# A scan layer with a mixture-of-experts layer: more places in the back phase, and a new order of the engines' work

## The reference

```python
h = layernorm(x) * (1 + ca) + sa
u = causal_conv(h, conv_w) + conv_b            # 4 taps, per channel
x_dbl = u @ xproj_w.T                          # dt (128), B (16), C (16)
delta = softplus(dt @ dtproj_w.T + dtproj_b)
# for each of 16 states n, in order of time:
#   h_n = exp(delta * A_n) * h_n + delta * B_n * u ;  y += C_n * h_n
x1 = x + ga * (y + u * D_skip)
h2 = layernorm(x1) * (1 + cb) + sb
# the router picks 2 of 8 experts for each row; scores = softmax of the two logits
out = x1 + gb * sum over the two experts of score_e * (silu(h2 @ Wup_e.T + bup_e) @ Wdown_e.T + bdown_e)
```

## Time and profile before

| | us |
|---|---|
| median of the three runs | 1313.03 |
| the profiled execution | 1310.42 |
| its span | 1308.7 |
| last scan of the front phase begins | about 1132 |
| last PE instruction ends | 1292.5 |

### The profile page before, as it was taken

How to read it: one execution, slowest core, us unless ns; L and a number is a source line. 1 busy time by engine, 2 the same in 40 slices (tenths; PEclk the granted TensorE clock), 3 DMA queues, 4 the chain that set the end, 5 groups by cost and what they waited for, 6 DMA issues and landing times. The chain is left out here.

```text
span 1308.7 us, 19847 instructions
## 1 busy us (share of the span) xinstructions
PE 1120.7 (86%) x5556; PEld 753.5 (58%) x5556; DVE 1110.2 (85%) x1562; ACT 877.6 (67%) x1684; POOL 916.8 (70%) x788
## 2 busy tenths in 40 slices
PE   8979778767769988898889998989889698999994
PEld 4467655445546656565557674656566465666551
DVE  4898899999988999899789998999889998853145
ACT  4864887948658975897598669976788474453231
POOL 2576686788778878888898767988887877423211
PEclk9999969757979999999999998999999789999997
DMA  6576443123224325233444521442541345785575
GB/s 213 182 262 218 121 158 101 49 73 139 82 93 121 129 66 153 94 130 96 140 119 132 145 64 60 143 137 72 155 121 66 115 143 183 232 285 185 153 232 171
DMA packets 104739, 181.02 MB, mean 138 GB/s; under 512 B 24864, under 2 KB 33056, under 8 KB 103608
## 3 DMA queue, kind: packets, MB, share of 16 engines
q1 hardware_dynamic: 91432, 141.33, 35.2%
q0 software_dynamic: 13200, 38.43, 7.7%
HBM read 116.34 MB, written 68.86 MB: 142 GB/s over the span
## 5 line engine op out<-in xcount | busy, mean ns | idle before, releaser
L1247 POOL TENSOR_TENSOR DB<-DU,BR 128x1024 f32<-128x1024 f32 x222 | 523.3, 2365 | 125.2 <-DVE H L1677 107.8
L2014 PE MATMUL pb<-ID,H 128*128 128x128 f32 x2048 | 323.8, 294 | 86.8 <-DVE ACC L1702 63.5
L1465 ACT ACTIVATE pb<-DELP,AN 128x512 f32<-128x512 f32 x448 | 305.7, 687 | 135.5 <-DVE H L1677 127.0
L1702 DVE SCALAR_TENSOR_TENSOR ACC<-pb,CTM,ACC 128x512 f32<-128x512 f32 x512 | 373.5, 730 | 13.9 <-PE pb L2014 13.4
L2014 PEld LDWEIGHTS pb<-ID,H 128*128 128x128 f32 x2048 | 254.2, 151 | 173.5 <-DVE ACC L1702 67.6
L1677 DVE TENSOR_TENSOR_SCAN H<-pb,DB 128x512 f32<-128x512 f32 x256 | 310.9, 1215 | 35.1 <-ACT pb L1465 17.3
L1677 DVE TENSOR_TENSOR_SCAN H<-pb,ST,DB 128x512 f32<-128x512 f32 x192 | 244.9, 1275 | 12.4 <-ACT pb L1465 9.1
L1232 POOL DMA_INDIRECT ydr<-YO,SCR x85 | 89.9, 1058 | 145.6 <-ACT YO L1547 129.7
L1547 ACT ACTIVATE YO<-pb,SCR 128x512 f32<-128x512 f32 x85 | 58.1, 683 | 71.5 <-PE pb L2117 71.1
L2087 PE MATMUL pb<-WU,XTS 128*128 x340 | 99.5, 417 | 0.0
L2112 PE MATMUL pb<-WD,GT 128*128 x170 | 98.4, 661 | 0.0
(11 more groups left out here) (251 smaller groups left out, 1731.9 us busy)
## 6 DMA issues: line engine op xcount, KB each, us to landing
BR<-bscr SPq DMA_DIRECT2D x112, 256.0 KB
XS<-xdr SPq DMA_DIRECT2D x85, 256.0 KB
DU<-ydr SPq DMA_DIRECT2D x64, 256.0 KB
xdr<-ZZ SPq DMA_DIRECT2D x37, 264.0 KB, 5.3
ACC<-in_x SPq DMA_DIRECT2D x16, 512.0 KB, 3.5
DU<-in_x SPq DMA_DIRECT2D x7, 1024.0 KB, 5.6
x1s<-ACC SPq DMA_DIRECT2D x24, 256.0 KB, 2.2
DELP<-x1s SPq DMA_DIRECT2D x24, 256.0 KB, 3.5
```

The source lines that it names most:

```text
L1247: eng.tensor_tensor(DB[:, i % NDB:i % NDB + 2], DU[:, c % 2, r:r + 2], BR[:, n % 2:n % 2 + 1].to_broadcast([128, 2, CT]), ALU.mult).then_i ...
L1465: eng.activation(DA[i % NDA][:], DEL[:, c % 2, r], ACT.Exp, scale=AN[:, r, n:n + 1]).then_inc(S["da"], 1)
L1702: eng.scalar_tensor_tensor(out=acc, in0=banks[bank_of["flip", c, n, r]][:], scalar=1.0 if n < 0 else CTM[:, c % 2, j, st:st + 1], in1=acc, ...
L2014: t = eng.transpose(b[:, dt * 128:dt * 128 + 128], src[:, dt, r * 128:r * 128 + 128], ID[:])
```

## The change

The rows get four places in place of two, and x1 gets eight in place of four; the new places are in the half of `DU` and `DEL` that belongs to chunk 7. A first use of a new place waits for the last `dbu` or `da` of chunk 7; later uses wait for `fin` of block b - 4 and `out` of block b - 8. Loads and stores of an x1 place now count on one semaphore. No instruction on an engine is added or removed.

```diff
         def x1_tile(g, t):
...
-            return DEL[:, (NC - 2) % 2, back_no(g, t) % 4]
+            r = back_no(g, t) % 8
+            return DEL[:, x1_chunk(r) % 2, r % 4]
         def z_tile(g, t, way):
-            return DU[:, (NC - 2) % 2, 2 * (back_no(g, t) % 2) + way]
+            r = back_no(g, t) % 4
+            return DU[:, z_chunk(r) % 2, 2 * (r % 2) + way]
         def turn_of_z(g, t):
-            return S[f"d_g{back_no(g, t) % 2}"], back_no(g, t) // 2
+            return S[f"d_g{back_no(g, t) % 4}"], back_no(g, t) // 4
         def turn_of(g, t):
             r = back_no(g, t)
-            return S[f"d_v{r % 4}"], S[f"d_p{r % 4}"], r // 4
+            return S[f"d_p{r % 8}"], sum(32 if x < 4 * (NC - 2) else 16 for x in range(r % 8, r, 8))
...
-                        eng.wait_ge(S["fin"], b - 1)
+                        eng.wait_ge(S["fin"], b - 3)
                     elif way == 0:
-                        eng.wait_ge(S["dbu"], slot(NC - 2, NS - 1, 3) + 1)
+                        eng.wait_ge(S["dbu"], slot(z_chunk(b), NS - 1, 3) + 1)
...
-                        eng.wait_ge(S["da"], slot(NC - 2, NS - 1, 3) + 1)
+                        eng.wait_ge(S["da"], slot(x1_chunk(back_no(g, t)), NS - 1, 3) + 1)
```

More of the change, by code:

```diff
@@ L74 @@
[L74 to L79, removed]
@@ L230 @@
-        "out": (15832, 15864, 16023, 16166, 16413, 16479, 16541, 16606, 16750, 16839, 16928, 17036, 17144, 17267, 17346, 17472,
[5 rows of a table removed]
+        "del": (-4, -3, 1852, 1865, 1938, 1991, 3640, 3651, 3662, 3725, 5712, 5756, 5769, 5782, 8053, 8062, 8089, 8135, 9980,
[5 rows of a table added]
+        "gbt": (175,),
+        "gbm": (6,),
+        "gbk": (-30,),
+        "gbb": (181,),
+        "gbe": (24,),
+        "gbs": (23,),
+        "bdh": (151,),
+        "bdl": (178,),
+        "gbl": (175, 181, 16710, 17603),
+        "dg2": (10,),
@@ new lines @@
+        "rowz": (232, 260),
+        "rowy": (238, 244, 250, 267, 273, 279),
+        "rcq": (237, 314),
+        "rt": (777, 873),
+        "mod": (766, 862),
+        "ldw": (329, 339, 492, 641, 782, 939, 1093, 1253),
[7 rows of a table added]
+        "skx": (174, 177, 179, 183),
+        "skp": (185, 187, 189, 191),
+        "skc": (89, 115, 138, 144),
+        "flip_": (2154, 2162, 2170, 2173, 4202, 4211, 4213, 4222, 6246, 6252, 6263, 6265, 8300, 8303, 8310, 8312, 10345, 10354,
+        10357, 10366, 12396, 12398, 12405, 12407, 14438, 14442, 14446, 14455),
@@ L236 @@
+        "out": (15918, 15922, 16401, 16437, 16724, 16743, 16762, 16774, 16998, 17041, 17181, 17200, 17315, 17395, 17545, 17615,
[5 rows of a table added]
 }
@@ L264 @@
+    "cpe": "6324324426464434644422262223",
+    "skx": "2563",
+    "dtr": "4366623",
+    "ftr": "32334334643443632234433263643443",
+    "r1": "2333643344623446",
+    "r2": "4342246344223246",
+    "hb": "42336442322463224334336626632323",
+    "rk": "343346424",
+    "xt": "2333344336464336242232224462666623643446366266442662246333642432324424262423463423636",
+    "gt": "66362333622466266443464322243463636336264242",
 }
@@ L693, in adaln_kernel @@
                      "d_bdn", "d_xa0", "d_xa1", "d_xp", "d_dtp", "d_bw", "d_br0", "d_br1", "d_gs",
-                     "d_gb", "d_w", "d_zi", "d_sc", "d_xl0", "d_xl1", "d_xl2", "d_xl3", "d_zr", "d_y0", "d_y1", "d_y2", *(f"d_{x}{r}" for x, n in (("g", 2), ("v", 4), ("p", 4)) for r in range(n)), "d_x10", "d_x11",
+                     "d_gb", "d_w", "d_zi", "d_sc", "d_xl0", "d_xl1", "d_xl2", "d_xl3", "d_zr", "d_y0", "d_y1", "d_y2", *(f"d_{x}{r}" for x, n in (("g", 4), ("p", 8)) for r in range(n)), "d_x10", "d_x11",
                      "d_x12", "d_x13"):
@@ L772, in pair_end, with x1_chunk, z_chunk @@
             return tile_no(g, tiles_of(g, p - pair_no(g, 0))[-1])
+        def x1_chunk(r):
+            return NC - 2 if r < 4 else NC - 1
+        def z_chunk(r):
+            return NC - 2 if r < 2 else NC - 1
         def x1_tile(g, t):
@@ L1001, in _ @@
                     cs, j = tokens(g)[t]
-                    loaded, stored, turn = turn_of(g, t)
-                    if turn:
-                        eng.wait_ge(stored, 16 * turn)
+                    moved, before = turn_of(g, t)
+                    if before:
+                        eng.wait_ge(moved, before)
                     else:
-                        eng.wait_ge(S["da"], slot(NC - 2, NS - 1, 3) + 1)
+                        eng.wait_ge(S["da"], slot(x1_chunk(back_no(g, t)), NS - 1, 3) + 1)
                     eng.wait_ge(S[f"d_x1{2 * (cs % 2) + j}"], 16 * (cs // 2 + 1))
-                    eng.dma_start(x1_tile(g, t), x1s[rows_of(g, t), :]).then_inc(loaded, 16)
+                    eng.dma_start(x1_tile(g, t), x1s[rows_of(g, t), :]).then_inc(moved, 16)
                 elif what == "out":
@@ L1011, in _ @@
                     eng.wait_ge(S["fin"], back_no(g, t) + 1)
-                    eng.dma_start(out[rows_of(g, t), :], x1_tile(g, t)).then_inc(turn_of(g, t)[1], 16)
+                    eng.dma_start(out[rows_of(g, t), :], x1_tile(g, t)).then_inc(turn_of(g, t)[0], 16)
             for g in range(len(GROUPS)):
                 for t in range(len(tokens(g))):
-                    _, stored, turn = turn_of(g, t)
-                    eng.wait_ge(stored, 16 * (turn + 1))
+                    moved, before = turn_of(g, t)
+                    eng.wait_ge(moved, before + (32 if bounced(tokens(g)[t][0]) else 16))
             eng.wait_ge(S["d_bw"], 16 * NC)
@@ L1826, in _ @@
                     if bounced(tokens(g)[t][0]):
-                        loaded, _, turn = turn_of(g, t)
-                        eng.wait_ge(loaded, 16 * (turn + 1))
+                        moved, before = turn_of(g, t)
+                        eng.wait_ge(moved, before + 16)
                     eng.tensor_tensor(to, to, z_tile(g, t, 0), ALU.add).then_inc(S["fin"], 1)
```

140 lines of the change are left out of this document (57 added, 83 removed), and 260 rows, old and new, of the table PLACES.

## The result

The changed kernel took 1322.91 us as the median of five runs (1320.86 to 1325.99), the kernel before 1310.73 beside it; the ratio is 1.0085 [1.0064, 1.0105]. That is 11 us slower by the ratio, and 12 between the two medians, where +3.3 was forecast. Run twice more beside the kernel before, it came to 1.0035 [1.0020, 1.0051] and 1.0084 [1.0056, 1.0111]. The interval of the second meets neither of the others, so one comparison of a kernel is less certain than its interval says. The mean of the three is 1.0068, +8.9 us: slower by over 0.5%, which the forecast had given a chance of 0.34. The median lies in the range of 1300 to 1328.

The account below looks back on a forecast made before the run. PE was taken as the bound from 1117.6 us, where group 7's first tile is transposed, to its end. 0 + 0 - 2.4 + 1.8 - 9.4 + 14.5 - 1.2 = +3.3 us, median 1316.3, range 1300 to 1328.

Parts of the forecast that it names:

- Step 1: Front phase up to chunk 7, bound by DVE: taken as 0, with some 9 us of scatter either way.
- step 3: Start of group 7's tiles (`xt7.0`): fewer POOL steps ahead of the last `zr`, -2.4 us, from -3.8 to +1.4.
- Step 2: Chunk 7: transposes moved as filler and two more tiles hide behind DVE or in holes, 0 us, -2 as other end.
- Step 4: PE's work from `xt7.0` on: the same 29 tiles, but four more transposes of a slot, +1.8 us.
- Steps 5 and 6: PE from `xt7.0` on: old waits go, -9.4 us; new waits for steps too close behind their operands come, +14.5 us.
- (b): New waits of PE at four `dn` close behind `gt`, for `ge`: `dn7.16`, `dn8.8`, `dn8.10` 1.2 us each, `dn7.10` 0.6.
- (c): New waits of PE at `up` directly behind its own `xt`: `up7.15`, `up8.9`, `up8.10` 0.8 us each, `up8.0` 0.4.
- Step 7: The end: the last `yg` follows at once with four places, the last `fin` earlier, -1.2 us, between -2 and 0.
- Rival 1: From `xt7.0` the dense new queue covers the new waits, 2 in place of 14.5: sum -9.2 us; chance 0.17.
- Rival 2: Rows load late around chunk 7's last transposes and router; DVE passes it on to PE: +11.3 us; chance 0.14.
- Rival 3: Waits around the last router drop PE's clock, four falls of 1.6 us: +9.7 us in all; chance 0.08.
- Rival 4: DVE's waits before chunk 7 differ: shorter, 1307.3 us and below, chance 0.15; or longer, 1325, chance 0.08.

Follow-up runs that it names:

- places_only: Kernel before with its order untouched and only the new places, for blocks 16 to 31: ratio 0.9995.
- front_b_back_a: Changed kernel with the old order up to the first scan of chunk 7 and the new order from there on: ratio 1.0054 against the kernel before.
- late_a: Kernel before with new places for blocks 16 to 31, and the new order only from the first transpose of group 8 (`xt8.0`) on: ratio 1.0008.
- gt_moved: Kernel before with new places for blocks 16 to 31, PE's `gt` steps of group 8 mostly moved later, behind one `up` more: ratio 0.9990.
- dq_moved: Kernel before with new places for blocks 16 to 31; in group 8 four `dq` moved directly ahead of `gt`, ACT's `ye` behind `th`: ratio 0.9969.
- after_tail_moved: Changed kernel with only PE's queue mended at the end (`r1`, `rk8`, some `xt`, `up`, `gt` moved): ratio 1.0039 against the kernel before.
- after_tail_both: Changed kernel with PE's and ACT's queues both mended from `dn7.11` on, a `dq` put into gaps ahead of `gt`: ratio 0.9996 against the kernel before.
- after_spread: Changed kernel with four `dbu` of chunk 4 moved forward on POOL, among group 3's sixteen indirect DMAs: ratio 1.0059 against the kernel before.
- front_a_back_b: Kernel before with the new order up to the first scan of chunk 7 and its own order from there on: ratio 1.0134.
- early_a: Kernel before with the new order only up to the scan of chunk 4, step 4, its own order behind: ratio 1.0030.

## Why the prediction was wrong in its first step and right behind it

The fronts that have one order up to chunk 7, start of the first scan of a chunk in us, mean and range:

| | old order | new order | difference |
|---|---|---|---|
| chunk 4 | 558.9 (556.7 to 561.3) | 563.9 (562.6 to 565.6) | +5.0 |
| chunk 5 | 698.4 (697.0 to 700.8) | 709.4 (707.8 to 710.9) | +11.0 |
| chunk 6 | 829.0 (827.2 to 832.1) | 838.6 (837.2 to 840.3) | +9.6 |
| chunk 7 | 973.5 (970.3 to 976.4) | 977.4 (974.7 to 980.6) | +3.9 |

(Old: before, places_only, front_b_back_a, late_a, gt_moved, dq_moved. New: after three times, after_tail_moved, after_tail_both, and for chunk 4 after_spread too. front_a_back_b is left out for its seam; up to chunk 6 it has 565.7, 710.9 and 838.6.)

**Step 1**, the front phase put at 0 without a row, is the one that failed. "I know of no row that says whether the new order meets fewer waits, so I take 0": the first pair gave +10.3, just outside the 9 that I had called the bound, the mean of the traces +3.9. So the first pair's number owes much to chance, and the lasting part is a loss that the step did not have. Two things were missed. The scatter of one and the same order is itself 6 us, so a part of the 10.3 was this pair of executions. And there was a row: POOL's wait of 3.44 us behind seven `zr`. I used it as a bound of step 3, for group 7, and did not look whether the new queue puts such a row of DMAs elsewhere. It does, in chunk 4: DVE idles 20.7 us there (mean of five) in place of 14.6 (of six), and put alone into the old order nearly the same thing costs 10.2 us. In the new order it costs less in the end, since chunks 5 and 6 are 7.1 us shorter. In part that may be work put off: 607 instructions of PE in chunk 6 in place of 663, some two to three tiles, which chunk 7 then hides. Why mending chunk 4 in the new order wins nothing is not settled; the joined orders have seams of their own. Ahead of chunk 4 the new order loses 5.0 us, 2.4 of it already by the middle of chunk 0 (106.4 against 104.0, means of the same traces), and early_a shows that this stays. Which waits make these 5 us I did not find out; so where the front's loss lies is shown, and why only for chunk 4.

**Step 2** held. In the first half of chunk 7 PE is busy 64.6 us and no longer 62.1, at a granted clock of 1.00 and no longer 0.92, and the half takes 74.2 in place of 73.4: two more tiles cost 0.8 at most, the faster transposes bring nothing. That two tiles more or less don't count is seen in front_b_back_a too, which has them done ahead and starts `xt7.0` at the same distance (146.4 us behind chunk 7's start, the changed kernel 146.1).

**Step 3** held by its sign: 147.4 became 146.1, -1.3 us for -2.4. **Step 4**: PE is busy 167.1 us from `xt7.0` to its end in place of 165.5, +1.6 for +1.8.

**Steps 5 and 6** held nearly wait by wait. The view is the waits of PE of the kernel after from 1126.7 us on, which answers to the earlier trace rows:

```profile
PE pb L2096 <- ACT XTS L1534: 3.7, 5, 0.9
PE pb L2122 <- ACT YO L1558: 3.6, 4, 1.3
PE pb L2112 <- DVE TH L1846: 3.1, 3, 1.5
PE pb L2122 <- ACT GT L1550: 2.1, 2, 1.3
PE pb L2044 <- ACT XH L1508: 1.6, 1, 1.6
PE pb L2068 <- POOL NM L1171: 1.0, 1, 1.0
```

The `gt` (L2112) wait 1.47, 1.03 and 0.60: 3.1 us, forecast 3.1. `dn` (L2122) at the four places of (b) 4.4, forecast 4.2; two of these end with `ye` and not with `ge`, so the releaser was wrong and the size right. `up` (L2096) at the four places of (c) 3.0, forecast 2.8. `dn7.17` 0.84, forecast 0.9. `r1` and `rk` 2.6, forecast 3.5. A wait of 0.66 before `up7.0` and one of 0.40 before `dn7.15` I had not seen. In all 15.0 us are idle; 9.3 of before are gone: +5.7 for +5.1.

**Step 7** held: the last `yg` follow each other at once (the last four loads of SP's timeline), and 14.2 us lie between PE's end and the end of the span in place of 16.1. That is -1.9 for -1.2; DVE's steps of the last two blocks, six from 1315.94 on, now stand without a gap of 0.2 us or more.

```profile
1312.48 1.94 SPq L1009 DMA_DIRECT2D DU<-ydr  x4
```

```profile
1315.94 0.69 DVE L1825 TENSOR_TENSOR DU<-DU 128x512 f32<-128x512 f32 x1 [5.87 <-DMA DU<-ydr]
```

**The rivals.** Rival 1, that the waits are covered, is refuted by the table of waits, and dq_moved and after_tail_both show what a covered queue would have brought. Rival 2 is not seen: the transposes end 210.5 us behind chunk 7's start, but PE idles only 0.7 us between `xt7.0` and there, and DVE has no wait for a load in it. Rival 3 happened in part. In the third trace of the changed kernel PE falls to the lower of its two levels behind the waits for `r1` (1.58) and `rk` (1.02), which the first trace has as well without it; its timeline there:

```profile
1211.37 0.39 PE L2068 MATMUL pb<-NM,UT 128*128 128x8 f32 x2 [1.02 <-POOL NM L1171]
...
1213.16 2.08 PE L2098 MATMUL pb<-WU,XTS 128*128 x4
...
1221.10 1.12 PE L2123 MATMUL pb<-WD,GT 128*128 x2
```

Four matmuls of L2098 take 2.08 us there in place of 1.13, and the granted clock from 1213 to 1219 us is 0.51, where the first trace has 1.00 in the same stretch (columns as in the earlier trace rows, third trace, then first):

```profile
1213.00:1219.00 6.00, 6.00 (x10) 3.00 (x11) 5.33 (x19) 0.60 (x1) 4.08 (x4) 0.51 0.39 144
1213.00:1219.00 6.00, 6.00 (x17) 3.08 (x18) 5.37 (x18) 1.07 (x2) 4.09 (x4) 1.00 0.41 152
```

From `xt7.0` to `xt8.0` this trace takes 120.6 us against 118.6, at 0.967 and 0.986 of the clock. Of the seven traces with the new back phase as it is, three have the 120.6, and four 118.6 to 119.0. By the rule of the Trainium skill's "TensorE: Matmul & The Clock Gate", section "HAM oscillation — how this bites in real kernels", gaps of waiting send the engine back (its own case has longer waits, one behind each block of work); the traces agree for three of seven, at 2 us, one fall more and not the four of rival 3. With this the back phase is 344.4 us in the mean of the seven, against 339.1 in the four traces with the old one: +5.3, of which the steps give +4.0 and the falls 0.8 (three of seven at 2 us); the rest is within the scatter of these traces (342.4 to 346.5). Rival 4, another front, came true on its longer side, at +3.9 and not at +9. Rival 5, that the places do nothing, is wrong by the 1 to 2 us of step 7: from PE's end to the end of the span lie 14.0 to 15.6 us in the kernels with new places, and 15.9 to 16.9 in the four without.

So +3.9 in front and +5.3 behind are +9.2 us, and the three ratios say +8.9.

## What to carry to other kernels

When a queue is laid out anew over the whole kernel, walk every stretch of it for the one or two patterns that the old trace shows to be dear, and not only the stretch at the end. Here the pattern was more than seven indirect DMAs of POOL in a row ahead of a step that another engine waits for. Where an engine is full to the end, the sum of its waits, taken place by place from the old trace, gave the cost within 1 us here; but to take a wait away, put work between the producer and every step that needs it, on each queue that it passes, and look which buffer the next step would write. And judge half a per cent from several traces: the same order came out 6 us apart.
